# First expert weights loaded and split earlier; tokens scattered in three waves to one region of rows per expert

## The reference, cut to what matters

```python
h = einsum('bnd,ed->bne', patches(x), proj_w) + proj_b
h = h + attn(layernorm(h))            # 12 heads of 64, quantised q, k, probs, v, out
x = layernorm(h)
top = argmax(einsum('bte,en->btn', x, Wg) + bg)                 # 4 experts
g = gelu(einsum('bte,neh->nbth', x, W1) + b1)                   # 192 -> 768
y = einsum('nbth,nhe->nbte', g, W2) + b2                        # 768 -> 192
out = h + y[top]
```

## Time and profile before

| | |
|---|---|
| median of 3 runs | 196.86 us (196.61 to 201.48) |
| the profiled execution | 194.78 us, span 193.0 us |
| mean granted clock of TensorE | 0.804 |
| PE, DVE, ACT, POOL busy | 146.5, 142.3, 115.0, 46.7 us |

### The profile page before, as it was taken

How to read it: one execution, slowest core, us unless ns; L and a number is a source line. 1 busy time by engine, 2 the same in 40 slices (tenths; PEclk the granted TensorE clock), 3 DMA queues, 4 the chain that set the end, 5 groups by cost and what they waited for, 6 DMA issues and landing times.

```text
span 193.0 us, 4994 instructions
## 1 busy us (share of the span) xinstructions
PE 146.5 (76%) x1794; PEld 113.0 (59%) x1794; DVE 142.3 (74%) x418; ACT 115.0 (60%) x220; POOL 46.7 (24%) x91
## 2 busy tenths in 40 slices
PE   0698898189988799856956588606559999999950
PEld 0698777045556456644544457406448788888830
DVE  3248657855879989999999987876113899898970
ACT  8933675047999779998775764720025556565710
POOL 2013123790000102020202211408730042423232
PEclk9999999655899855998585555555966999999996
DMA  4799900899960000404040400003439800000000
GB/s 124 293 290 288 393 6 0 285 237 215 366 217 2 3 0 5 126 0 122 4 122 3 124 5 0 0 0 135 174 138 273 292 33 23 25 33 20 27 20 21
DMA packets 9463, 21.45 MB, mean 111 GB/s; under 512 B 1744, under 2 KB 5210, under 8 KB 9440
## 3 DMA queue, kind: packets, MB, share of 16 engines
q1 hardware_dynamic: 8288, 18.17, 30.8%
q0 software_dynamic: 1152, 2.97, 4.2%
HBM read 15.39 MB, written 6.04 MB: 111 GB/s over the span
## 4 chain that ended last, share of the span: by engine, by line
PE 39%; DVE 28%; issue 11%; ACT 7%; DMA 7%; SPq 3%; POOL 2%; DVEq 0%; ACTq 0%; POOLq 0%
PE lin_bank L1096 12%; DMA patches<-in_patches 7%; PE head_bank L1108 6%; PE lin_bank L896 4%; PE lin_bank L900 3%; PE head_bank L1115 3%; DVE w L648 3%; DVE mx L688 2%; DVE dif L696 2%; PE head_bank L869 2%; DVE den L691 2%; PE score_bank L1068 2%; DVE aint L718 2%; PE score_bank L968 2%; DVE oT L581 2%
## 5 line engine op out<-in xcount | busy, mean ns | idle before, releaser
L544 ACT ACTIVATE q<-lin_bank,b 128x128 f32<-128x128 f32 x72 | 25.1, 367 | 33.0 <-PE lin_bank L1096 32.3
L1096 PE MATMUL lin_bank<-q,w 128*128 128x128 f16 x360 | 32.1, 230 | 4.0 <-issue 3.7
L1096 PEld LDWEIGHTS lin_bank<-q,w 128*128 x360 | 25.8, 103 | 8.1 <-issue 4.7
L396 POOL TENSOR_TENSOR rstd<-veps,nhalf 128x1 f32<-128x1 f32 x9 | 8.6, 963 | 69.4 <-DVE veps L599 69.4
L1108 PE MATMUL head_bank<-early,q 128*128 x72 | 22.6, 332 | 0.4 <-DVE q L851 0.3
L869 PE MATMUL head_bank<-proj_w,patches 128*128 128x192 f32 x72 | 15.3, 373 | 7.2 <-DMA patches<-in_patches 7.2
L414 POOL DMA_INDIRECT out<-q,patches x12 | 11.8, 988 | 36.0 <-DVE q L833 35.7
L919 PE MATMUL score_bank<-k,q 128*128 128x36 bf16 x256 | 9.7, 186 | 14.2 <-DVE dif L696 10.7
L896 PE MATMUL lin_bank<-ww1q,xqT 96*128 96x384 bf16 x64 | 19.0, 445 | 0.0
L451 ACT ACTIVATE vint<-lin_bank,fac 128x768 int16<-128x768 f32 x16 | 14.5, 904 | 7.2 <-PE lin_bank L896 7.1
L869 PEld LDWEIGHTS head_bank<-proj_w,patches 128*128 128x128 f32 x72 | 14.2, 223 | 7.5 <-issue 6.6
(11 more groups left out here) (134 smaller groups left out, 329.1 us busy)
## 6 DMA issues: line engine op xcount, KB each, us to landing
patches<-in_patches SPq DMA_DIRECT2D x9, 384.0 KB, 11.6
slots<-blank SPq DMA_DIRECT2D x12, 226.0 KB, 9.6
patches<-slots SPq DMA_DIRECT2D x12, 226.0 KB, 5.5
patches<-in_w SPq DMA_DIRECT2D x4, 576.0 KB, 3.7
early<-in_ww SPq DMA_DIRECT2D x3, 576.0 KB, 11.0
patches<-in_w SPq DMA_DIRECT2D x1, 1536.0 KB, 8.4
patches<-in_w SPq DMA_DIRECT2D x2, 768.0 KB, 12.9
proj_w<-in_proj_w SPq DMA_DIRECT2D x1, 576.0 KB, 4.3
```

The source lines that it names most:

```text
L544: a.activation(g[:, j % 2, m], up_bank[n % 4][:, 0:P], ACT.Gelu, scale=1.0 / WSCALE, bias=b1[:, bass.ds(e, 1), m]).then_inc(g_ok, 1)
L1096: last = mm(up_bank[n % 4][:, 0:P], up_weights(j, part, m), xT[:, j % 3, piece], start=x == 0, stop=x == len(PASSES) - 1)
```

## The change

* The up matrices are loaded expert by expert (`w1_in[e]`), each when the two patch tiles under it have been embedded. The first six high halves are made on ACT ahead of the attention loop, their low halves on DVE at the end of steps 0 and 1 (three each), and halves 6 and 7 in the two steps after. Nothing is left of `w1` for steps 6 to 14. The down matrices keep their steps.
* Routing goes in three waves of tiles (0 to 4, 5 and 6, 7 and 8). `choose(w)` and `place_wave(w)` on DVE and `count(w)` on PE stand inside steps 17, 18, 20 and 21 for the first two waves and behind the loop for the last.
* A token's slot no longer depends on how many tokens the other experts get: the table has a region of 1152 rows for each expert, and expert `e` begins at row 1152 `e` (`region`). The table grows from 1536 to 4992 rows, all blanked, in three transfers in place of twelve.
* POOL scatters tiles 0 to 2 between the `rstd` of tile 6 and that of tile 7, the others after the last `rstd`.
* SP reads the first row of each slot tile from `slot_row` into registers and loads `xs` from there, in order. Picking is gone: all 12 tiles are transposed from loaded rows.
* POOL adds the attention's bias tile by tile in the embedding; the gates of tiles 0 to 2 move in front of a step's scores.

```diff
+    SLOTS = (NEXP - 1) * T + SLOT_TILES * P
+    WAVES = [(0, 5), (5, 7), (7, TT)]
...
-        EARLY = 2 * NEXP
+        EARLY, AHEAD = 2 * NEXP, 6
...
-            return [n for n in range(len(SPLITS)) if i == (6 + n if n < EARLY else 7 + n)]
...
+            return [n for n in range(AHEAD, len(SPLITS)) if i == (1 + n - AHEAD if n < EARLY else 7 + n)]
+        CHOOSE_AT, COUNT_AT, PLACE_AT = {17: 0, 20: 1}, {17: 0, 21: 1}, {18: 0, 21: 1}
...
-            sp.wait_ge(emb_ps, TT)
-            sp.dma_start(w1f[:, :, 0], w1_d[0:P]).then_inc(w1_in, 16)
-            for half in range(2):
-                sp.dma_start(w1f[half * TAIL:(half + 1) * TAIL, :, 1], w1_d[P:E]).then_inc(w1_in, 16)
+            for e in range(NEXP):
+                sp.wait_ge(emb_ps, 2 * e + 2)
+                sp.dma_start(w1f[:, e, 0], w1_d[0:P, e]).then_inc(w1_in[e], 16)
+                for half in range(2):
+                    sp.dma_start(w1f[half * TAIL:(half + 1) * TAIL, e, 1], w1_d[P:E, e]).then_inc(w1_in[e], 16)
...
-            for j in range(SLOT_TILES):
-                sp.dma_start(slots_d[j * P:(j + 1) * P, :], blank[:]).then_inc(blank_out, 16)
+            tiles = SLOTS // P // BLANKS
+            for b in range(BLANKS):
+                sp.dma_start(slots_d[b * tiles * P:(b + 1) * tiles * P, :].rearrange("(j p) n -> p j n", p=P),
+                             blank[:].unsqueeze(1).to_broadcast([P, tiles, ROW])).then_inc(blank_out, 16)
...
+            sp.wait_ge(slot_row_ok, 1)
+            at = nc.values_load_multi_w_load_instructions(slot_row[0:1, :], engines=[mybir.EngineType.SP], min_val=0,
+                                                          max_val=SLOTS - P, skip_runtime_bounds_check_because=(
+                                                              "each tile lies in its expert's region or behind it"))[1]
             sp.wait_ge(scattered, 16 * TT)
-            for j in [PICKED] + [j for j in range(SLOT_TILES) if j != PICKED]:
-                sp.dma_start(xs[:, j], slots_d[j * P:(j + 1) * P, :]).then_inc(xs_in[j], 16)
+            for j in range(SLOT_TILES):
+                sp.dma_start(xs[:, j], slots_d[bass.ds(at[j], P), :]).then_inc(xs_in[j], 16)
...
+            def add_bias(t):
+                if t == 0:
+                    pool.wait_ge(bb2_in, 16)
+                pool.wait_ge(norm_ok, t + 1)
+                gp.tensor_tensor(row[:, t, 0:E], row[:, t, 0:E], bb2[:], ALU.add).then_inc(hb_ok, 1)
...
+                if t >= 1:
+                    add_bias(t - 1)
+            add_bias(TT - 1)
...
+                gp.memset(tile_row[:, j:j + 1], float(j * P - T)).then_inc(const_ok, 1)
+            for e in range(NEXP):
+                gp.memset(region[:, e:e + 1], float(e * TT)).then_inc(const_ok, 1)
+            def scale(t):
...
-            pool.wait_ge(ex_ok, PAIRS)
-            step(gp.iota(slot_int, pattern=[[1, PICKED * P]], base=0, channel_multiplier=0))
-            gp.tensor_copy(slot_no, slot_int).then_inc(slot_no_ok, 1)
...
+            def scatter(w, t0, t1):
+                pool.wait_ge(blank_out, 16 * BLANKS)
+                pool.wait_ge(const_ok, NCONST)
+                pool.wait_ge(xlo_ok, t1)
+                pool.wait_ge(xhi_ok, 2 * t1)
+                pool.wait_ge(slot_ok, w + 1)
+                for t in range(t0, t1):
+                    gp.indirect_dma_start(out=slots_d, out_offset=bass.IndirectOffsetOnAxis(ap=slot[:, t:t + 1], axis=0),
+                                          in_=row[:, t, :], in_offset=None,
+                                          bounds_check=SLOTS - 1, oob_is_err=False).then_inc(scattered, 16)
             for t in range(TT):
-                gp.indirect_dma_start(out=slots_d, out_offset=bass.IndirectOffsetOnAxis(ap=slot[:, t:t + 1], axis=0),
-                                      in_=row[:, t, :], in_offset=None,
-                                      bounds_check=SLOTS - 1, oob_is_err=False).then_inc(scattered, 16)
+                scale(t)
+                if t == 6:
+                    scatter(0, 0, 3)
+            scatter(0, 3, 5)
+            scatter(1, 5, 7)
+            scatter(2, 7, TT)
...
+            for n in range(AHEAD):
+                split_high(n)
...
+            def choose(w):
+                t0, t1 = WAVES[w]
+                n, ts = t1 - t0, slice(t0, t1)
+                if w == 0:
+                    dve.wait_ge(gate_in, 32)
+                    dve.wait_ge(const_ok, NCONST)
+                dve.wait_ge(gate_ps, t1)
+                if w == 0:
+                    rstep(d.tensor_tensor(logit[:, 0:EARLY_GATES], gate_early[:, 0:EARLY_GATES],
+                                          each_tile(gate_b[:], EARLY_GATES), ALU.add))
+                late_ts = slice(max(t0, EARLY_GATES), t1)
+                d.tensor_tensor(logit[:, late_ts], gate_late[:, late_ts],
+                                each_tile(gate_b[:], t1 - late_ts.start), ALU.add).then_inc(logit_ok, 1)
+                dve.wait_ge(logit_ok, w + 1)
+                rstep(d.tensor_reduce(best[:, ts], logit[:, ts], AX.X, ALU.max))
+                rstep(d.tensor_tensor(isbest[:, ts], logit[:, ts], each_expert(best[:, ts], n), ALU.is_equal))
+                rstep(d.tensor_tensor(logit[:, ts], isbest[:, ts], each_tile(prio[:], n), ALU.mult))
+                rstep(d.tensor_reduce(best[:, ts], logit[:, ts], AX.X, ALU.max))
+                d.tensor_tensor(onehot[:, ts], logit[:, ts], each_expert(best[:, ts], n), ALU.is_equal).then_inc(onehot_ok, 1)
+            def place_wave(w):
+                ts = slice(*WAVES[w])
+                counts = count_bank[w]
+                dve.wait_ge(onehot_ok, w + 1)
+                dve.wait_ge(count_ps, w + 1)
+                rstep(d.tensor_tensor(place[:, ts], counts[:, ts], onehot[:, ts], ALU.mult))
+                rstep(d.tensor_reduce(slot_f[:, ts], place[:, ts], AX.X, ALU.add))
+                d.tensor_copy(slot[:, ts], slot_f[:, ts]).then_inc(slot_ok, 1)
...
+                if i < 2:
+                    for n in range(i * AHEAD // 2, (i + 1) * AHEAD // 2):
+                        split_low(n)
                 for n in splits_at(i - 1):
                     split_low(n)
+                if i in CHOOSE_AT:
+                    choose(CHOOSE_AT[i])
+                if i in PLACE_AT:
+                    place_wave(PLACE_AT[i])
...
+            LAST = len(WAVES) - 1
+            choose(LAST)
+            place_wave(LAST)
+            rstep(d.tensor_scalar(ntile[:], count_bank[LAST][:, TT], 1.0 / P, (P - 1) / 2 / P, ALU.mult, ALU.add))
             rstep(d.tensor_tensor(prod[:], earlier[:], each_tile(ntile[:], NEXP), ALU.mult))
             rstep(d.tensor_reduce(first[:], prod[:], AX.X, ALU.add))
-            rstep(d.scalar_tensor_tensor(place[:], each_tile(first[:]), float(P), counts[:, 0:TT], ALU.mult, ALU.add))
-            rstep(d.tensor_tensor(place[:], place[:], onehot[:, 0:TT], ALU.mult))
-            rstep(d.tensor_reduce(slot_f[:], place[:], AX.X, ALU.add))
-            d.tensor_copy(slot[:], slot_f[:]).then_inc(slot_ok, 1)
             rstep(d.tensor_tensor(started[:], each_expert(tile_no[:], SLOT_TILES), each_tile(first[:], SLOT_TILES),
                                   ALU.is_ge))
             rstep(d.tensor_reduce(expert_f[:], started[:], AX.X, ALU.add))
+            rstep(d.tensor_tensor(start_of[:], started[:], each_tile(first[:], SLOT_TILES), ALU.mult))
+            rstep(d.tensor_reduce(first_of[:], start_of[:], AX.X, ALU.max))
+            rstep(d.scalar_tensor_tensor(at_row[:], expert_f[:], float(T), tile_row[:], ALU.mult, ALU.add))
+            d.scalar_tensor_tensor(slot_row[:], first_of[:], -float(P), at_row[:], ALU.mult, ALU.add).then_inc(slot_row_ok, 1)
...
-            def pick(j):
-                for t in range(TT):
-                    d.tensor_scalar(picked[:, j, t], slot_no[:, j * P:(j + 1) * P], slot_f[:, t:t + 1], None,
-                                    ALU.is_equal).then_inc(picked_ok, 1)
...
+            slots_T(0)
+            slots_T(1)
...
+                if t == TT - 2:
+                    pe.wait_ge(logit_ok, 1)
...
+                bank = gate_early if t < EARLY_GATES else gate_late
+                for w, (t0, t1) in enumerate(WAVES):
+                    if w and t0 <= t < t1:
+                        pe.wait_ge(logit_ok, w)
...
+            def count(w):
+                t0, t1 = WAVES[w]
+                end = t1 + (t1 == TT)
+                pe.wait_ge(onehot_ok, w + 1)
+                pe.wait_ge(const_ok, NCONST)
+                pe.wait_ge(lin_int, len(lin_order))
+                bank = count_bank[w]
+                mm(bank[:, t0:end], before[:], onehot[:, t0:end], start=True, stop=False)
+                for t in range(end - 1):
+                    s = max(t0, t + 1)
+                    mm(bank[:, s:end], ones[:], onehot[:, t:t + 1].to_broadcast([P, end - s, NEXP]), start=False, stop=False)
+                mm(bank[:, t0:t1], ones[:],
```

(18 more changed lines are left out.)

121 lines of the change are left out of this document (37 added, 84 removed).

## The result

The change made the kernel faster, and by more than was forecast: 187.32 us (median of 4, 186.3 to 188.26) against 196.74 us (195.13 to 201.48), ratio 0.9546, interval 0.946 to 0.9633. Timed again (experiment 7), the ratio was 0.9602 (0.9532 to 0.9671). The forecast was 195.3 with a range down to 190.5.

What follows compares the result with a forecast made beforehand. The prediction took DVE's low halves in the later score steps, then the loop's end and picking with its crawl, as bounds; 3.0 us gained in attention less 1.4 lost in routing took 196.86 to 195.3 us, range 190.5 to 200.0.

Steps and rivals of the forecast that it cites:

- The step that failed: Experts' start: before, steady at 143.2 us after picking and a crawl, worth 141.8 clean; changed, 143.2, so 1.4 us lost.
- The routing as a whole: From the loop's end to the experts' steady run: choosing in waves without picking loses 1.4 us.
- The three costs inside the loop: Steps 17 to 21: `choose(0)` before `oT` 1.6 us, `rstd` behind three scatters 2.3, `choose(1)` and `place_wave(1)` 2.1.
- The attention: Score steps: low halves leaving steps 7 to 14 gain 5.5 us, moved early they cost 2.5; 3.0 us gained.
- The cost of the early halves: Steps 0 to 3: low halves moved there on DVE outgrow its waits and cost 2.5 us, bounds 1.3 and 4.8.
- PE's waits for `dif` from 80 to 106 down from 4.7 us to about 1: Sign in the later score steps: PE waits less for DVE's differences, 4.7 us falling to about 1.
- From the last choice to the first up: Behind the loop: choice, count, placing, two scatters, loads and transposes, from 131.8 to 143.2 us.
- The blanks and the early gates: Blanking 4992 table rows (26 us) stays hidden; gates before the scores fit PE's room, 1.4 us if uncovered; costed at nothing.
- (a): Rival at the loop's end: `choose(0)` fits before the `oint` that `oT` needs, tail hidden, 6.0 us gained, 190.9; chance 0.2.
- (b): Rival at the experts' start: the crawl belongs to the first register-addressed matmuls and recurs, 2.0 us slower, 198.9; chance 0.15.
- (c): Rival in steps 18 to 22: scatters slow some six hand-overs by 2.4 to 4.2 us, 197.8 to 199.6; chance 0.15.
- The 0.24 us: Last two scatters: beside busy DVE, descriptor writing might take 0.24 us longer each, adding 0.5 us.

Runs made afterwards that it cites:

- experiment 7: The changed kernel again without an edit, timed beside the others and traced once more: 188.98 us, ratio 0.9602.
- experiment 4: The kernel before, unchanged, traced a second time: 195.37 us, one execution.
- Experiment 5: The kernel before with only the first four of POOL's nine scatters, the other five tiles' rows left out: 186.24 us, ratio 0.9548.
- experiment 6: The kernel before without picking, all twelve slot tiles loaded and transposed, nine scatters kept behind the routing: 197.46 us, ratio 1.0157.
- experiments 1 and 2: 1: kernel before with only the weights' part, 194.13 us, then 191.93, ratio 0.9821. 2: changed kernel with the weights' part put back, 191.34 us, ratio 0.9822.
- experiment 3: The kernel before with POOL's nine scatters held until PE had done the first slot tile's up matmuls: 204.42 us, one execution.
- experiment 10: The changed kernel with the second wave merged into the last, tiles 5 to 8 routed together behind the loop: 190.76 us, ratio 0.982.
- experiment 9: The changed kernel with two scatters, not three, between the two `rstd`, and the second slot tile transposed later: 186.63 us, ratio 0.9581.

## Why the forecast was wrong

The stretches, in us. "Before" is the mean over all traces with that program part, with their range; the last column is what was forecast for the difference.

| stretch | before | changed | difference | forecast |
|---|---|---|---|---|
| start of the span to last mx | 104.7 (6 traces, 103.6 to 106.4) | 102.4 (8 traces, 100.2 to 106.0) | -2.3 | -3.0 |
| last mx to `oT` | 8.9 | 10.1 | +1.1 | +1.6 |
| `oT` to `xn` of tile 7 | 5.9 | 7.4 | +1.5 | +2.3 |
| `xn` of tile 7 to last choice | 4.5 | 5.6 | +1.1 | +2.1 |
| last choice to last up | 58.9 (4 traces, 58.0 to 59.5) | 51.6 (3 traces, 51.3 to 52.1) | -7.3 | -4.6 |

**The step that failed** is "before, at 143.2 with 12 of slot tile 0's 60 matmuls done, which at 25 matmuls in 2.83 us are worth 1.4 us, so at 141.8 for a clean start" (a tile has 30 of them; 60 are those of both picked tiles), and the reading behind it, that picking and then a crawl set the start of the experts. From 141.8 to the last up at 183.8 are 42.0 us, but it takes 39.0 to 40.9 from the first to the last up in the nine traces in which PE waits for no load. In the first trace, where PE waited for no load either, the excess lies in the stretches of the second and third tile's `up`, 5.55 and 3.75 us where the changed kernel has 4.13 and 3.37. Without the crawl the first two tiles were done earlier and nothing was won by it, since PE ran dry behind them (experiment 4); what bound was POOL's nine scatters at 1.28 us each, SP's loads and the landing of the fourth tile. Experiment 5 takes five scatters away and gets 6.7 us in this stretch, experiment 6 takes the early start away and loses 3. The waves move seven scatters off this path: from the slots to the end of the last scatter it is 3.3 us, and was 12.6 to 12.9. The forecast had the same row of scatters in it and followed PE's side of the fork alone. In this stretch 2.7 us were missed: 1.8 are the 42.0 us in place of some 40.2, and 0.9 is that the trace read, with 58.0, was the shortest of the four. The routing as a whole was forecast to lose 1.4 us and gained 3.6 (7.3 - 3.7): 2.7 of these 5.0 us lie here, 2.3 in the next three costs.

**The three costs inside the loop** were right in mechanism and too large, 3.7 us for 6.0. `choose(0)` stands in front of `oT` and nothing hides it, but its operations on 20 values follow each other every 0.2 us, not every 0.23, and the clip overlaps the last: 1.1 for 1.6. The three scatters hold the `rstd`, in 3.8 us from 113.23 to 116.99 exactly as worked out, but `xn` waits 1.91 us where 0.44 were there already: 1.5 for 2.3. `choose(1)` and `place_wave(1)` took 1.07 and 0.46 us, but 0.19 us of DVE's idle time went, and the low half behind the two `row` operations started 0.54 us after them in place of 0.74: 1.1 for 2.1.

**The attention** came out near the forecast, but by luck in part, since the clock moves it by more than the forecast is worth. In the first pair of traces it looked like 6.2 us, and each removed half like a whole microsecond. But that trace of before had the half clock from 66.5 to 76.5 and again from 90.5 to 97, and that of after had the full clock from 48 to 95.5. Over fourteen traces the difference is 2.3, with ranges of 3 and 6 us. Three of the eight changed ones (105.95, 104.58 and 103.36) had a low mean granted clock, 0.76 to 0.79 where the other five had 0.82 to 0.84; those five alone give 101.1, a difference of 3.6. That fits experiments 1 and 2, where the weights' part alone and the routing's alone are 1.8% each, 3.5 us. The cost of the early halves was as forecast: in the first pair `mx` was 2.9 to 3.7 us late at pairs 3 to 6, for 2.5 and bounds of 1.3 to 4.8. ACT's high halves were hidden. The sign "PE's waits for `dif` from 80 to 106 down from 4.7 us to about 1" did not come: in the same steps they are 4.7 us still. The sentence "From 66 to 80, though, PE is busy for 13.6 of 14 us, so there a lighter DVE gains almost nothing" read a granted clock of 0.63 as a property of the program: at full clock PE has 3.4 us of room there.

**From the last choice to the first up** 11.4 us were forecast and 11.3 to 11.6 measured. The blanks and the early gates cost nothing that shows. The first `mx` starts at 38.8 us on average in the nine traces with loads by expert, at 38.3 in the other five; the kernel with the weights alone has it too (38.7 and 38.8), and no run separates the cause of this half microsecond.

**The rivals.** (a) did not happen: `xn` waited. (b), a crawl that belongs to register-addressed matmuls, is out: no other trace of the fourteen has one. (c), scatters that disturb their neighbours, is out too. The three costs inside the loop came out below a forecast that held nothing for it, so its 2.4 us or more find no room. In the second trace of the kernel before, 40 matmuls took 2.71 us at full clock beside three scatters with the DMA engines 0.50 busy, and the 31st started 1.75 us after the first, as in experiment 3 with no scatter beside it; this agrees with what the Trainium skill says in SBUF — State Buffer, section on SBUF's two separate sides, that a transfer and a computation do not slow each other. The 0.24 us that the prediction allowed for each of the last two scatters beside a busy VectorE did not come: they took 0.97 us each.

What this leaves: the stretches add up to 5.9 us of gain (7.3 + 2.3 - 3.7), or 7.2 with the five traces alone, while the two ratios, 0.9546 and 0.9602, are worth 8.9 and 7.8 us. The rest may be in how often an execution meets the half clock in its attention; that is not shown, and one or two traces a kernel are too few for it. Why the first trace crawled is open as well; it was seen once, and no experiment brought it back.

## What to carry to other kernels

* Where two chains join, an early start on one of them is worth only what the other leaves. Ask of every head start what the engine will do when it is used up: here 60 picked matmuls, and behind them 5.2 us of waiting for a table that POOL was still writing when they began. A crawl or a wait in front of such a join can be free.
* A stretch in which an engine is "full" at half its clock is no bound of the program. Read the clock's column before the busy column, and take a second trace before a difference of a few microseconds is explained.
* A row of equal steps on one queue (nine scatters, 1.28 us apart) is cut by moving steps to before the last input is known, as the waves do. Once it was spread here, four rearrangements only traded a wait ahead of it for one behind it.

## What the runs showed of the hardware

* An indirect transfer of 128 rows to the table takes 0.97 or 0.98 us on POOL in most cases, and the next one of a row starts 0.30 us later. The first of a kernel takes 1.19 to 1.28, and about one in six of the others 1.0 to 1.5; why is not shown. The data of the last had landed 2.7 to 2.9 us after that transfer's start (3.3 in one trace). On the profile's timeline the 0.97 us are POOL's alone: the Trainium skill, Perfetto Trace Analysis, section DMA Instruction — SWDGE (GPSIMD), says that such a record ends when the descriptors are made and not when the data have moved, and the chain, with 1.7 us between the two, agrees.
* The granted clock of one program differs between its executions by up to 30 us of half clock inside the attention, and this moved the last mx from 100.2 to 106.0 us. It fell at 66.4 us in the first trace of the kernel before and at 95.7 in that of the changed kernel, behind a microsecond in which PE was busy for 0.18 and for 0.13 us, but from 56 to 57 in the changed kernel PE was busy for 0.10 us and the clock stayed at 1.00, so no rule can be read from this.
* After a stretch with PE mostly idle, the full clock (1.00, 2.4 GHz) came back 1.9 us (experiment 10) to 5.6 us (experiment 9) after the first `up` matmul. A first `up` 1.0 us earlier behind the last mx (experiment 9) was followed by a run 0.4 to 0.8 us longer.
